# Selective-scan phase of a conv/Mamba kernel: twelve more state pairs a pass get c times B on ScalarE, and VectorE multiplies each by dx in one product of 384 columns

## The reference, cut to what matters

```python
def selective_scan(u, delta, A, B, C, D):
    A = jnp.clip(A, -5.0, 5.0)
    dA = jnp.einsum('bld,dn->bldn', delta, A)
    dB_u = jnp.einsum('bld,bld,bln->bldn', delta, u, B)
    c = jnp.concatenate([dA[:, 1:], jnp.zeros_like(dA[:, :1])], axis=1)
    c = jnp.flip(c, axis=1)
    c = jnp.cumsum(c, axis=1)
    c = jnp.exp(jnp.minimum(c, 15.0))
    c = jnp.flip(c, axis=1)
    x = jnp.cumsum(dB_u * c, axis=1) / (c + 1e-06)
    y = jnp.einsum('bldn,bln->bld', x, C)
    return y + u * D
```

## Time and profile before

| | |
|---|---|
| median of 3 runs | 19240.01 us (19239.32 to 19246.41) |
| profiled execution, its own time | 19243.72 us |
| its span | 19241.8 us |
| busy share of the span | PE 84%, PEld 43%, VectorE 93%, ScalarE 73%, GpSimd 79% |
| stretch of the height axis | 1755 to 9480 us |
| stretch of the width axis | 9616 to 17232 us |

### The profile page before, as it was taken

The page is one execution under the profiler, slowest core; times in us unless marked ns, Lnnn a source line. Parts: engine busy times, 40 slices in busy tenths (PEclk is TensorE's granted clock), DMA queues, the critical chain, the costliest instruction groups (busy, mean ns, idle before and its releaser), DMA issues. The chain is left out here.

```text
span 19241.8 us, 290646 instructions
## 1 busy us (share of the span) xinstructions
PE 16257.4 (84%) x60328; PEld 8303.8 (43%) x60424; DVE 17802.0 (93%) x48666; ACT 13962.1 (73%) x18390; POOL 15292.2 (79%) x10500
## 2 busy tenths in 40 slices
PE   5776888888888888888688888888888888887777
PEld 2223444444444444444344444444444444442222
DVE  4998999999999999999899999999999999984888
ACT  4665777777777777777577777777777777761666
POOL 1554999889888998888699999999999999970444
PEclk8998999999999999999899999999999999996999
DMA  1000000000000000000000000000000000000000
GB/s 33 13 13 12 11 11 11 11 11 11 11 11 11 11 11 11 11 11 11 12 11 11 11 11 11 11 11 11 11 11 11 11 11 11 11 10 20 10 12 11
DMA packets 778173, 227.53 MB, mean 12 GB/s; under 512 B 747760, under 2 KB 750476, under 8 KB 776332
## 3 DMA queue, kind: packets, MB, share of 16 engines
q1 hardware_dynamic: 776332, 206.79, 8.2%
HBM read 143.66 MB, written 62.97 MB: 11 GB/s over the span
## 5 line engine op out<-in xcount | busy, mean ns | idle before, releaser
L1222 POOL TENSOR_TENSOR h_sm<-h_sm,h_wr 128x768 f32<-128x768 f32 x2944 | 5400.3, 1834 | 755.2 <-DVE h_wr L1002 669.6
L1222 POOL TENSOR_TENSOR w_sm<-w_sm,w_wr 128x768 f32<-128x768 f32 x2944 | 5399.1, 1834 | 502.5 <-DVE w_wr L1002 404.6
L1386 PE MATMUL w_pz<-w_xr,w_tri 128*128 128x384 f32 x9984 | 4462.6, 530 | 788.2 <-DVE w_wr L1002 622.5
L1386 PE MATMUL h_pz<-h_xr,h_tri 128*128 128x384 f32 x9984 | 4424.7, 526 | 770.6 <-DVE h_wr L1002 604.5
L1002 DVE SCALAR_TENSOR_TENSOR h_wr<-h_pz,h_bct,h_rbuf 128x192 f32<-128x192 f32 x11776 | 4250.3, 407 | 171.9 <-PE h_pz L1386 171.2
L1002 DVE SCALAR_TENSOR_TENSOR w_wr<-w_pz,w_bct,w_rbuf 128x192 f32<-128x192 f32 x11776 | 4243.4, 408 | 96.1 <-PE w_pz L1386 95.5
L976 DVE SCALAR_TENSOR_TENSOR w_xr<-w_cbuf,w_bct,w_pdx 128x192 f32<-128x192 f32 x9984 | 3634.9, 405 | 76.0 <-issue 35.2
L976 DVE SCALAR_TENSOR_TENSOR h_xr<-h_cbuf,h_bct,h_pdx 128x192 f32<-128x192 f32 x9984 | 3632.6, 404 | 75.7 <-issue 35.2
L1098 ACT ACTIVATE h_cbuf<-h_pe_e,h_consts 128x1024 f32<-128x1024 f32 x2304 | 2526.1, 1112 | 1532.4 <-PE h_pe_e L1374 1332.1
L1098 ACT ACTIVATE w_cbuf<-w_pe_e,w_consts 128x1024 f32<-128x1024 f32 x2304 | 2526.1, 1112 | 1492.7 <-PE w_pe_e L1374 1305.1
L604 POOL TENSOR_TENSOR m_gv<-m_hs,m_cv 128x512 f32<-128x512 f32 x1024 | 1351.0, 1322 | 2240.9 <-DVE m_hs L468 2213.4
(11 more groups left out here) (355 smaller groups left out, 19595.9 us busy)
## 6 DMA issues: line engine op xcount, KB each, us to landing
h_lt<-pieces_s SPq DMA_DIRECT2D x512, 96.0 KB, 4.4
w_lt<-pieces_s SPq DMA_DIRECT2D x512, 96.0 KB, 4.3
pieces_s<-h_pieces SPq DMA_DIRECT2D x384, 48.0 KB, 2.1
pieces_s<-w_pieces SPq DMA_DIRECT2D x384, 48.0 KB, 2.1
h_xt<-first_s SPq DMA_DIRECT2D x34, 128.0 KB, 5.5
w_xt<-first_s SPq DMA_DIRECT2D x34, 128.0 KB, 3.1
m_u<-hn_s SPq DMA_DIRECT2D x32, 128.8 KB, 2.7
m_u<-slots_s SPq DMA_DIRECT2D x32, 128.8 KB, 2.6
```

The lines of the kernel that those rows point to most:

```text
L1222: tt(sm[:, g], sm[:, g], wr[:, u % 3], ALU.add).then_inc(s_add, 1)
L1386: t.matmul(pz[:, P % 2, 0:2 * DX], tri[:], x, start=True, stop=True).then_inc(s_z, 1)
```

## The change

A second list, `WIDE`, holds the 12 pairs a pass with P % 8 == 6; `SCALED` is `OTHER` and `WIDE` together, 30 pairs. ScalarE now scales the c of all 30 in place (`scale_c` walks `SCALED` in order). For a pair of `WIDE` VectorE waits for that scaling (`s_cb`) and then multiplies both states by dx, read from PSUM with a broadcast over the two states, in one `tensor_tensor` of 128x384 into `xr`. GpSimd's waits on `s_cb` count in `SCALED` now; everything else is as it was.

```diff
         OTHER = [P for P in range(PAIRS) if P % 8 == 7 or P % 16 == 11]
+        WIDE = [P for P in range(PAIRS) if P % 8 == 6]
+        SCALED = sorted(OTHER + WIDE)
         OWN = PAIRS - len(OTHER)
@@ product (VectorE)
                     if P % 8 == 0:
                         dve.wait_ge(s_c, T * GRP + 3 * ch + 3)
+                    if P in WIDE:
+                        dve.wait_ge(s_cb, T * len(SCALED) + SCALED.index(P) + 1)
+                        v.tensor_tensor(xr[:, P % 3, :].rearrange("p (m d) -> p m d", m=2),
+                                        cbuf[:, ch % 2, n % 16:n % 16 + 2, :],
+                                        pdx[:, g * DX:(g + 1) * DX].unsqueeze(1).broadcast_to([128, 2, DX]),
+                                        ALU.mult).then_inc(s_x, 1)
+                        return
                     for m in range(2):
@@ scale_c (ScalarE)
-                    for P in OTHER:
+                    for P in SCALED:
                         if P // 8 != ch:
                             continue
@@ product (GpSimd)
-                    pool.wait_ge(s_cb, T * len(OTHER) + OTHER.index(P) + 1)
+                    pool.wait_ge(s_cb, T * len(SCALED) + SCALED.index(P) + 1)
```

## The result

The changed kernel takes **19346.12 us** (median of 4 runs, 19340.07 to 19379.16) against 19241.79 us for the kernel before (4 runs): ratio 1.0056, 95% interval [1.0042, 1.0070]. It is slower by 104 us, where I had forecast no change; the time lies inside the range, near its upper end. The profiled execution is the slowest of the four, 33 us above the median, and 135.4 us above the profiled execution of before.

The account below looks back on a forecast made before the run. VectorE was taken to bound the kernel: per pass 5.5 x 0.18 = 0.99 us saved against 1.02 lost at pair 52, 4 us over 126 passes, offset by 4 in the last passes: 19240 us, no change; range 19120 to 19375.

Parts of the forecast that it names:

- VectorE sets the pace, and savings count only where it sets the next point: Both axes: VectorE busy 97 to 98%; an instruction removed saves its whole cost, except ahead of a wait.
- Pairs 14, 22 and 30: Steps 12 to about 31: their 0.18 us each is lost in waits of `gated`, weighting 22 and weighting 28 or `make_xc`.
- the late five: Pairs 62, 70, 78, 86 and 94: no VectorE wait behind them, 0.18 us each kept if TensorE can follow.
- pair 30's saving: Lost: height axis, weighting 28 waits 0.35 us; width axis, `make_xc` waits for `sig_x`, pushed back 0.35 us.
- Pair 6: Start of a pass: saving kept where weighting 5 doesn't wait; counted as half a pair.
- 0.18 us a pair: VectorE, each wide pair: two state instructions at 0.65 us become one product at 0.47 us, priced from the gate product.
- Rival 2: The wide product costs 0.55 us, saving only 0.10 a pair: 19295 us, chance 0.12; at 525 ns, 19278 us.
- The chain: ScalarE, c group 2 of chunk 5 to r group 0 of chunk 7: extra scalings make it 1.02 us later.
- The wait of weighting 52: VectorE waiting for TensorE's sums of pair 52: grows from 0.20 to 1.76 us, every pass but an axis's last.
- Rival 1: ScalarE's delay is absorbed and pairs 38, 46, 54 count: 19043 us, chance 0.12; without local waits too, 18964, chance 0.05.
- Pair 38: Its c product lies between step 35 and weighting 52: its 0.18 us only lengthens that wait, saving nothing.
- the sentence on GpSimd: GpSimd gets no work, its adds are not hurried before pair 52, and VectorE's later arrival gives it time; no cost.

Follow-up runs that it names:

- remedies: Changed kernel with the prefix scan issued before weighting 52 and seven extra 128x128 matmuls on TensorE at step 50; together 19213.12 us, ratio 0.9981 to the kernel before.
- pair 46 alone: Changed kernel with 46 as the only wide pair (`WIDE = [46]`); 19469.58 us, ratio 1.0119 to the kernel before.
- pair 54 alone: Changed kernel with 54 as the only wide pair (`WIDE = [54]`); 19446.71 us, ratio 1.0106 to the kernel before.

## Why the prediction was wrong

- **VectorE sets the pace, and savings count only where it sets the next point: right.** Pairs 14, 22 and 30 gave nothing, alone or in company; the late five gave their 0.18 each. On the width axis pair 30's saving goes at weighting 29, which now waits 0.12 us, and not at `make_xc`, as I had argued. Pair 6: in the 30 even passes of each axis between 1 and 61, which have no branch ahead of them, weighting 0 to 8 takes 9.75 us in every kernel without it and 9.56 to 9.57 in every kernel with it, so its whole 0.18 is kept there. In nearly all odd passes, behind the loop's branch, TensorE is at half clock at steps 0 to 2, before the change too; their means lie from 10.7 to 11.8 us with pair 6 or without, and what it gives in them can't be read. Half a pair, as I had counted, is the part that is sure.
- **0.18 us a pair: right.** The product starts 0.46 us before the next instruction, VectorE's rows at step 12, and `gated` waits 0.35 us as said (0.34):

```profile
4203.83 0.54 DVE L979 TENSOR_TENSOR h_xr<-h_cbuf,h_pdx 128x384 f32<-128x384 f32 x1
4204.29 0.73 DVE L1011 SCALAR_TENSOR_TENSOR h_wr<-h_pz,h_bct,h_rbuf 128x192 f32<-128x192 f32 x2
4205.37 0.56 DVE L963 TENSOR_TENSOR h_yz<-h_pf,h_gate 128x384 f32<-128x384 f32 x1 [0.35 <-PE h_pf L1363]
```

  The row was the right price, not the 525 ns of the Trainium skill's page "VectorE: DVE Perf Modes", section "The TRN2 errata". Rival 2 is out.
- **The chain gets 1.02 us later: right**, 1.05. The wait of weighting 52 was to be 1.76 and is 1.64 in pass 12, at full clock. Rival 1 is out.
- **Pair 38 was absorbed at weighting 37**, not at 52; the place was wrong, the amount nearly right (0.15 of the 0.18 us).
- **The step that failed** is the sentence on GpSimd, "its adds are not hurried before pair 52; VectorE's later arrival there even gives it time", and with it the silent assumption that what stands behind weighting 52 costs what it did. I moved VectorE by a microsecond relative to GpSimd and TensorE and priced only the move. Two terms were missing from the sum. The scan behind the add: from 52 to 53 1.89 / 1.81 us in place of 1.52, so 0.37 and 0.29. TensorE's halved clock after a pause of 2.61 us in place of 1.35: from 51 to 52 3.08 / 3.15 in place of 2.83 at full clock, 0.25 and 0.32, and from 53 to 64 0.27 and 0.17 over the 13.26 that its own passes at full clock take. Together 0.89 and 0.78 us a pass, 105 us over 63 passes of each axis. They belong beside the 120.6 us that the two axes lost in the traced execution; of the rest, step 34 of the width axis is 24 us (19.02 us from 32 to 48, against 18.64 in its passes without half clock there), and the start of a pass gave some back. That the medians differ by 104 us, nearly the same as 105, is luck. The remedies show that both terms are real: with both the kernel is 36 us below the one before, in place of 104 above. These 140 us don't size the two terms, because the scan, placed ahead of the weighting, then also fills a wait that stood there anyway: from weighting 52 to 53 it takes 0.87 us, where it took 1.52 even before the change.
- The trace of before held the evidence for the first: the mean of the scan's group (970 ns) hides it, the longest of 64 (2449 ns) shows it, and the scan stood 0.07 us ahead of an add. For the second it held nothing at this place, but it did at another: at the start of nearly every odd pass, behind the loop's branch, TensorE pauses for 2.8 to 3.7 us, and half clock follows in 22 and 30 of the 31 odd passes between 1 and 61 of the two axes; in the even ones, where the pause is 0.78 us, it never does. The chance that a longer pause of TensorE costs more than the pause should have widened the upper side.

## What to carry to other kernels

When a change shifts one engine against another, the shift isn't the whole price: look at what the shifted instruction now meets on the shared resources, and check each neighbour that is ahead by less than the shift. An instruction whose longest duration is far above its median can be a collision that is waiting for a small delay. And before widening an edit to every place of a pattern, ask of each place whether its saving is kept and whether its cost is hidden: here six of twelve pairs bring everything (140 us), two cost all of it and more, and four bring nothing that can be measured.

## What the hardware did that I had not expected

- The cost of a collision isn't monotonic in the delay: 0.33 us of delay cost 1.2 us at the scan (pass 13 with pair 46 alone), 1.02 us cost 0.5 us (pass 12 with all twelve).
- A pause of TensorE of 2.6 us was followed by a half clock in most passes but not in all (pass 12 and pass 20 above, both 2.61 us). After a pause of about 1.90 us it came in 23 passes of the height axis with pair 46 alone, and in 8 of the width axis; after one of 2.04 us in 24 and 54 with pair 54 alone. So the length of the pause doesn't decide it by itself, and what does stays open. The pause of 1.35 us at pair 52 was never followed by one. Seven small matmuls in the pause prevented it in all passes.
- At step 34 of the width axis TensorE fell to half clock in no pass of the kernel before and of the one with pair 54 alone, and in 4 to 29 passes of all others. The longest pause shortly before, at step 32, is 0.85 or 0.86 us in every pass of all thirteen traces, with half clocks or without, before the change too. What decides it stays open. A pass that it strikes takes 20.31 us from 32 to 48 in place of 18.64 (both remedies), so in 4 to 29 passes it costs some 7 to 45 us, and several totals came above their expectation by part of that.
